# Attention units of a fused attention and MoE layer: the softmax normalisation of one unit issued after the score work of the next

## The reference, cut to what matters

```python
scores = jnp.einsum('bqhd,bkhd->bhqk', q, k)
scores = jnp.where(mask[None, None], -jnp.inf, scores)
attn = jax.nn.softmax(scores / np.sqrt(Dh).astype(np.float32), axis=-1)
ctx = jnp.einsum('bhqk,bkhd->bqhd', attn, v).reshape(b, s, H * Dh)
x = _layernorm(x + ctx @ Wo)
x = _layernorm(x + ffn(x))      # relu experts, top 4 of 16 by gate
```

## Time and profile before

| what | us |
|---|---|
| median of 3 runs | 4984.84 |
| lowest and highest of them | 4658.09, 5114.94 |
| the profiled execution | 4416.83 |
| its span, slowest core | 4415.3 |
| its spans over the 8 cores | 4390.4 to 4415.3 |

### The profile page before, as it was taken

How to read it: one execution, slowest core, us unless ns; L and a number is a source line. 1 busy time by engine, 2 the same in 40 slices (tenths; PEclk the granted TensorE clock), 3 DMA queues, 4 the chain that set the end, 5 groups by cost and what they waited for, 6 DMA issues and landing times.

```text
span 4415.3 us, 48483 instructions; the slowest of 8 cores (4390.4 to 4415.3 us)
## 1 busy us (share of the span) xinstructions
PE 3864.2 (88%) x20016; PEld 1914.3 (43%) x20016; DVE 1010.4 (23%) x2242; ACT 813.1 (18%) x1212; POOL 223.4 (5%) x427
## 2 busy tenths in 40 slices
PE   2776786677678899999999999999999999999997
PEld 2443453444454444444444444444444444444443
DVE  2224224313423420211221121121121112112112
ACT  0234324323434211001001101100100100110114
POOL 0000000000000001001001000100100100100000
PEclk7887887788788999999999999999999999999998
DMA  8101101110133155236326425524623632642552
GB/s 149 29 1 29 29 6 24 29 29 1 29 56 98 27 89 101 43 67 105 58 48 105 77 39 95 96 40 75 105 48 57 105 68 38 105 79 40 92 96 77
DMA packets 65130, 274.46 MB, mean 62 GB/s; under 512 B 7406, under 2 KB 7918, under 8 KB 60816
## 3 DMA queue, kind: packets, MB, share of 16 engines
q0 software_dynamic: 60704, 253.99, 33.7%
q1 hardware_dynamic: 4208, 17.37, 1.2%
HBM read 516.84 MB, written 8.39 MB: 119 GB/s over the span
## 4 chain that ended last, share of the span: by engine, by line
PE 77%; DVE 7%; DMA 6%; ACT 5%; issue 4%; DVEq 0%; ACTq 0%; POOL 0%; POOLq 0%; SPq 0%
PE PP L941 30%; PE PP L860 28%; PE PP L515 5%; PE PP L495 5%; DMA ar<-w1x 3%; PE PP L463 3%; ACT ar L346 3%; DVE ar L331 3%; PE PP L590 3%; PE PP L422 2%; DMA ar<-xs 2%; DVE ar L323 1%; DMA ar<-xo 1%; PE PP L310 1%; DVE ar L401 1%
## 5 line engine op out<-in xcount | busy, mean ns | idle before, releaser
L941 PE MATMUL PP<-ar 128*128 128x512 bf16 x6336 | 1395.7, 384 | 47.9 <-DVE ar L919 45.1
L860 PE MATMUL PP<-ar 128*128 128x512 bf16 x6336 | 1387.9, 379 | 20.7 <-DMA ar<-w1x 17.0
L941 PEld LDWEIGHTS PP<-ar 128*128 128x128 bf16 x6336 | 623.9, 99 | 819.1 <-issue 91.2
L860 PEld LDWEIGHTS PP<-ar 128*128 128x128 bf16 x6336 | 611.6, 98 | 793.7 <-issue 80.0
L874 ACT ACTIVATE ar<-PP,b_sb 128x512 bf16<-128x512 f32 x396 | 250.7, 684 | 2531.5 <-PE PP L860 2531.5
L964 DVE SCALAR_TENSOR_TENSOR ar<-PP,ar 128x512 f32<-128x512 f32 x576 | 357.8, 684 | 1035.5 <-PE PP L941 1025.0
L422 PE MATMUL PP<-ar 128*128 128x128 bf16 x1152 | 109.8, 256 | 309.2 <-DVE ar L401 246.2
L886 DVE TENSOR_TENSOR ar<-ar 128x1024 bf16<-128x1024 bf16 x176 | 121.9, 693 | 1117.1 <-ACT ar L874 1117.1
L422 PEld LDWEIGHTS PP<-ar 128*128 128x128 bf16 x1152 | 84.2, 113 | 335.8 <-issue 335.8
L515 PE MATMUL PP<-ar 128*128 128x256 bf16 x2048 | 224.9, 273 | 0.0
L495 PE MATMUL PP<-ar 128*128 128x512 bf16 x1024 | 222.3, 379 | 0.0
(11 more groups left out here) (100 smaller groups left out, 1203.2 us busy)
## 6 DMA issues: line engine op xcount, KB each, us to landing
ar<-w1x POOLq DMA_DIRECT2D x198, 512.0 KB, 6.2
ar<-w2x POOLq DMA_DIRECT2D x198, 512.0 KB, 8.2
ar<-wqkv POOLq DMA_DIRECT2D x8, 2048.0 KB, 16.0
ar<-wqkv POOLq DMA_DIRECT2D x8, 1024.0 KB, 22.0
ar<-xs POOLq DMA_DIRECT2D x4, 2048.0 KB, 36.8
ar<-wo POOLq DMA_DIRECT2D x2, 4096.0 KB, 41.9
ar<-xo SPq DMA_DIRECT2D x8, 1024.0 KB, 9.5
out<-ar SPq DMA_DIRECT2D x16, 512.0 KB, 3.3
```

Source lines behind the costliest of these rows:

```text
L860: e.matmul(PA[:, bank * 512:(bank + 1) * 512], W1c[pp][:, dc * 128:(dc + 1) * 128], xhat[:, dc * 1024 + nt * 512: dc * 1024 + (nt + 1) * 512],
L941: e.matmul(PP[:, bank * 512:(bank + 1) * 512], H_sb[:, fc * 1024 + ti * 128: fc * 1024 + (ti + 1) * 128], W2c[:, fc * 2048 + (bank % 4) * ...
```

## The change

The normalisation is cut out of `emit_unit_exp` and becomes a function of its own, `emit_unit_norm`. `norm_pend` holds the one unit whose normalisation is still to be emitted. A step of the loop now emits: front of unit u, normalisation of unit u-1, back of unit u-3, exp of unit u. The last unit of a group is normalised after the next group's Q projection and ahead of the emptying of `pend`; the last of all after the loops. The instructions and their number stay, buffers too.

```diff
@@ emit_unit_exp
         sc_state["free"][usc] = sb.mark("ac")
-        sb.wait("vector", "ac", sc_state["free"][usc])
+        return sc_state["free"][usc]
+
+    def emit_unit_norm(ent):
+        up, kc = ent["up"], kcount(ent["i"])
+        sb.wait("vector", "ac", ent["exp_ac"])
         sb.do("vector", (lambda e, up=up: e.reciprocal(linv_sp[up], lsum_sp[up])), "dv", 1)
...
-        return (hA, mpnA, mpnB)
+        ent["mpn"] = (hA, mpnA, mpnB)
@@ for g, behind the Q projection
+        if norm_pend["e"] is not None:
+            emit_unit_norm(norm_pend["e"])
+            norm_pend["e"] = None
         while pend:
-            emit_unit_back(*pend.pop(0))
+            emit_unit_back(pend.pop(0))
@@ for g, for jl, for i
                 mstat = emit_unit_front(g, jl, i, up)
+                if norm_pend["e"] is not None:
+                    emit_unit_norm(norm_pend["e"])
+                    norm_pend["e"] = None
                 if len(pend) >= npar:
-                    emit_unit_back(*pend.pop(0))
-                mpn = emit_unit_exp(g, jl, i, up, mstat)
-                pend.append((g, jl, i, up, mpn))
+                    emit_unit_back(pend.pop(0))
+                ent = {"g": g, "jl": jl, "i": i, "up": up, "mpn": None}
+                ent["exp_ac"] = emit_unit_exp(g, jl, i, up, mstat)
+                pend.append(ent)
+                norm_pend["e"] = ent
                 uc += 1
```

More of the change, by code:

```diff
@@ L288, in build_nc @@
     sc_free_ac = 0
-    unit_par = 0
     pend = []
+    norm_pend = {"e": None}
     cmx = st_sb[:, 4:8]
@@ L369, in emit_unit_exp, with emit_unit_back @@
             mpnB = mpnA
-        return (hA, mpnA, mpnB)
-    def emit_unit_back(g, jl, i, up, mpn):
+        ent["mpn"] = (hA, mpnA, mpnB)
+    def emit_unit_back(ent):
         nonlocal pt_free_pe, ctx_evac_ac
+        g, jl, i, up = ent["g"], ent["jl"], ent["i"], ent["up"]
         kc = kcount(i)
         nkb = kc // 128
-        hA, mpnA, mpnB = mpn
+        hA, mpnA, mpnB = ent["mpn"]
         ev_marks = []
```

## The result

The changed kernel takes 1.0053 times the time of the kernel before, with a 95% interval of 1.0031 to 1.0076, from 14 runs of each. On the profiled execution of 4416.83 us that is 23 us more, between 14 and 34. The profiled execution of the changed kernel took 4438.83 us, its slowest core 4437.3 us.

What follows compares the result with a forecast made beforehand. DVE, ACT and PE wait on each other in the attention units, none full. Gains of 3.6 and losses of 5.5 us a group net 1.9 lost, about 15 us in eight groups: 4416.8 becomes 4432 us, range 4400 to 4465.

Steps and rivals of the forecast that it cites:

- The chain: Between units: next scores wait for front's end, reciprocal, ACT scaling, ACT copy and V product; net 1.9 us lost a group.
- step 0: Gap between unit 0's front and unit 1's: 1.24 us before, nothing left in it after; gain 1.2 us a group.
- step 3: Gap between unit 3's front and unit 4's: gain 0.6 us a group.
- step 10: Gap after unit 10's front, the longest at 4.48 us: becomes about 3.8, gain 0.7 (0.3 to 1.1).
- step 7: Gap after unit 7's front: 3.70 us by ACT's path against 3.02 before, loss 0.7 us.
- step 9: Gap after unit 9's front: loss 0.9 us a group (0.6 to 1.3, by the clock).
- step 6: Gap after unit 6's front: comes out even, no gain or loss.
- The group's end: Behind the last Q copy: unit 15's scaling delays the first block copy, PE has nothing else; loss 1.0 us.
- Rival C: Attention gaps: DVE copy paths shorter than reckoned, small gain of 2 to 4 us a group, about 4395 us; chance 0.22.
- Rival A: Attention units: DVE's wait for exp is simply gone, 4234 us, 4.1% less; chance 0.06.
- Rival B: Steps 3 to 15: PE's transposes end after the front, 88 us on top, 4520 us, 2.3% more; chance 0.09.
- Rival D: At 5 of 16 steps DVE still waits for exp, the score buffer being shared; in the sum, no chance given.

Runs made afterwards that it cites:

- copies off it: Changed kernel with the back of unit u-3 (copies of transposed blocks) emitted ahead of the normalisation of unit u-1: ratio 0.9854, 4346.05 us.
- scores off it: Changed kernel with PE's V product of unit u-3 put behind the scores of unit u+1: ratio 0.971, 4277.86 us.
- a shorter link: Changed kernel with ScalarE scaling a quarter of the row in place of a half, VectorE the rest: ratio 1.0012, 4438.90 us.
- the fastest kernel: Changed kernel with block copies ahead of normalisation, score buffers alternating, V product late, last normalisation ahead of the Q projection: ratio 0.9525, 4203.90 us.

## Why the prediction was right and where it was wrong

**The wait removed** was costed rightly: the wait for exp ahead of the reciprocal fell from 182.6 to 19.8 us, "below 20" by the prediction.

**The chain** is confirmed by its links in the timeline and by five runs: copies off it (0.9854), scores off it (0.971), a shorter link (1.0012), and the last two edits made on the kernel before, where the late V product gains less (0.9889) and the shorter scaling loses (1.0018). The signs it named came in: L323's wait 157 us higher (120 or more), copies behind the front's end, units 78.3 us (76 to 82), clock 0.61, experts not moved (2780 us from the first product of L941 to the last, 2782 before).

**The sum** was 15 us where 23 were measured, inside the forecast's own range of 4400 to 4465 us. By terms, in the group read: the gain of step 0 was 0.9 us, not 1.2, because the scores of unit 1 wait for their PSUM bank until L327 of unit 0 is done (PE idles 1.20 us there); step 3 gained 0.5, not 0.6; step 10 gained 0.3, not 0.7, for PE's V product of 16 blocks took 1.81 us in the timeline (1.05 before), past the slow end of the 0.85 to 1.7 us allowed; step 7 lost 0.9, not 0.7; step 9 lost 0.5, not 0.9, and step 6, put down as even, gained 0.5. All gaps together lost 0.5 us where 0.1 was worked out, and the start of the Q projection behind the last front lost 1.2, not 0.8. That the fronts last as long as before was nearly so (0.2 us more in the mean of seven groups). The group's end cost the 1.0 us worked out. A term was missing: the dense work behind the units. The Q projection takes 15.8 us in the mean of seven groups in place of 15.5, and in one group the stretch behind it took 12.67 us, at the lower clock. Counted over the seven groups, the units give 1.8 us, the Q projection 0.3, the stretch behind it 1.5 and the K projection 0.1, in sum 3.7 us a group against the 1.9 of the prediction. The last group, counted as the others, lost 3.9 (84.98 to 88.88 us). The output projection starts 30 us later (1401.2 us in place of 1370.9), and the stretch from there to the first product of L941, in the experts, gave 7 back; why that stretch is shorter was not tried.

**Rival C**, a small gain, did not come: steps 0, 1, 3 and 10 gained 2.7 us in the group read where 3.5 were worked out.

**The time on record** failed at its last step, "I add the 15 us to that median". The base of that sum, the median of three runs at 4984.84 us, was the wrong one: the median of the changed kernel came out at 4441.29 us, 559 us lower. What the runs showed in its place is that the 15 us belonged on the profiled execution, whose granted clock was alike on all eight cores (0.929 to 0.934): the sum of 4432 us made against its 4416.8 was 9 us off that median. The prediction had seen that the three runs were 457 us apart and 568 us above the profiled execution in their median. The spread of the three runs was taken for the range, which cut off the place where the profiled execution itself lay. Its lower end should have been under 4416.

**Rival A**, the wait simply gone, was wrong for this kernel and right in sign for one with another order on PE: there the same change gains 1.8%, less than half of A's 4.1%. The rule weighed for it, of the Trainium skill's page Perfetto Trace Analysis, Optimization Strategy (find the gaps of the engine that one optimizes for and make what it waits for come sooner), brings a gain only if the next thing it waits for is not right behind (to optimize the engine with the highest occupancy first is said in the section ahead of it, Identifying the Most-Contended Engine); the trace here disagrees with the gain and agrees with the choice of engine, since in the fastest kernel DVE is busy for 84% of the window. The 1.2 us by which the scores were early belong to step 7, which the prediction took for the longest wait; the longest, 3.33 us, is that of step 10. **Rival B**, transposes late by 88 us, did not come: DVE's copies wait 146.0 us for transposes where they waited 135.8. **Rival D**, the shared buffer, is in the sum and shows as 22.4 us of wait; removing it alone gained nothing in the whole time.

## What to carry to other kernels

When an instruction is put off so that an engine need not wait, list what stands behind it on every engine, not only on the one that waited: here the scaling that was put off held ACT's copy, this PE's V product, and this the scores for which the freed engine waits next. Waits of 180 us in all hid the scores: in the gap of step 7 they were only 1.2 us early, and the change itself made their chain longer. So removing it was worth nothing until the chain was cut, and then the same change was worth 1.8%. And state the effect of a change against the execution whose trace you read, not against the median of a few runs that lie hundreds of microseconds above it.

## What the runs showed of the hardware that was not expected

The lower clock of PE can follow the waiting loop into the dense work behind it, and small shifts decide it. Behind the Q projection PE idles 2.22 us in the changed kernel, in six groups without a consequence (granted clock 1.00 in that stretch) and in one with 3 us more (0.66); with the score buffers in turn, where only the units ahead are 2 us shorter, the clock fell in all seven groups, and it cost 2.6 us in that stretch and 1.1 in the K projection behind it. In the eight groups where it fell, the Q projection ahead had taken 14.6 to 14.9 us, and in the six others 15.8 to 16.2; why the two go together was not tried. Before, with 1.18 us idle at that place, the stretch took 8.63 or 8.64 us every time. The Q projection itself, the same 64 matmuls, takes 15.5 us before, 14.6 to 16.2 after, and 13.81 in every group of the fastest kernel; the granted clock in the units is 0.62, 0.61 and 0.73 in these three. So closing waits in the units can bring something in the dense work too, and no sum of durations had it in it. The prediction's rule from the Trainium skill, TensorE: Matmul & The Clock Gate, Part 1, that the clock goes by how busy the array has been, agrees with this order of the three. But the mean over the units does not foretell the Q projection: the changed kernel with the late V product has 0.63 in its units and takes 13.81 us as well, and copies first with buffers in turn has 0.67 and takes 15.4 to 15.5.

In the changed kernel with the late V product (4277.86 us) and in the one with all four edits (4203.90 us) a wait for exp stays in sight at step 8, where the front is short. The gap there is 4.74 us in the first: DVE waits 2.26 us for the exp of unit 7 ahead of its reciprocal and 1.13 us for the exp of unit 8 in the shared buffer. It is 2.22 us in the second, with 0.60 us of waiting for the exp of unit 7. The reciprocal of unit 7 stands behind a front of only 1.2 us there, while the exp of 2048 columns lasts 2.0 us. Putting the normalisation off by one unit covers exp only where the next front is the longer.
